# Moving the run-time branch of a fused attention and mixture-of-experts kernel ahead of the weight folds

## The reference

```
k_ids = jnp.arange(lk)[None, None, :]
qs = seg_id[:, :, None]
good = (k_ids <= qs) & (k_ids >= qs - LOOKBACK)
scores = jnp.where(good[:, None, :, :], scores, NEG)
attn = jax.nn.softmax(scores, axis=-1)
```

## Time and profile before

| | us |
|---|---|
| three runs, in order | 519.15, 522.25, 518.19 |
| median of the runs | 519.15 |
| the profiled execution | 518.47 |
| span of its profile, first to last instruction | 516.7 |
| TensorE busy | 499.3 |
| VectorE busy | 249.6 |
| ScalarE busy | 185.2 |
| GpSimd busy | 60.3 |

### The profile page before, as it was taken

One profiled execution on the slowest core, in us unless ns is written; L12 is line 12 of the kernel. 1 busy time (PEld: TensorE's weight loads), 2 busy tenths in 40 slices (PEclk: granted clock), 3 DMA queues, 4 the chain that ended last, 5 costly groups with the idle time before them and its releaser, 6 DMA issues.

```text
span 516.7 us, 10575 instructions
## 1 busy us (share of the span) xinstructions
PE 499.3 (97%) x3878; PEld 363.5 (70%) x3878; DVE 249.6 (48%) x549; ACT 185.2 (36%) x534; POOL 60.3 (12%) x71
## 2 busy tenths in 40 slices
PE   8699999999999999997999998999999999999997
PEld 7476777777877788885798885555555555556886
DVE  2565876876766668987553221222222222222334
ACT  2157567566566444444411111112112112121110
POOL 2000000000000122132006500000000000000650
PEclk9799999999999999999999999999999999999999
DMA  9800000000991009400523162777877877852241
GB/s 289 321 22 1 20 22 1 19 20 15 362 410 48 2 17 408 189 0 1 209 98 126 70 220 90 269 264 279 306 270 283 310 261 291 301 210 82 80 125 41
DMA packets 24455, 82.05 MB, mean 159 GB/s; under 512 B 2880, under 2 KB 16512, under 8 KB 20320
## 3 DMA queue, kind: packets, MB, share of 16 engines
q1 hardware_dynamic: 21536, 75.93, 40.3%
q0 software_dynamic: 1536, 4.20, 2.6%
q10 hardware_dynamic: 1344, 1.38, 0.8%
HBM read 73.10 MB, written 8.39 MB: 158 GB/s over the span
## 4 chain that ended last, share of the span: by engine, by line
PE 88%; DVE 6%; issue 3%; ACT 2%; POOL 0%; DVEq 0%; ACTq 0%; POOLq 0%
PE ps L1808 17%; PE ps L1721 12%; PE ps L1317 12%; PE ps L1832 9%; PE ps L1733 6%; PE ps L1396 5%; PE ps L1346 5%; PE ps L1365 5%; PE ps L1488 3%; PE ps L1384 3%; ACT w_routed L1096 1%; PE ps L1322 1%; PE ps L1498 1%; PE ps L1677 1%; PE ps L1338 1%
## 5 line engine op out<-in xcount | busy, mean ns | idle before, releaser
L1808 PE MATMUL ps<-w_routed,xnT 128*64 x320 | 93.8, 436 | 1.6 <-DVE x_sb L967 1.6
L1721 PE MATMUL ps<-xT_all,w_shared 128*128 128x256 f32 x320 | 75.7, 380 | 0.0
L1808 PEld LDWEIGHTS ps<-w_routed,xnT 128*64 128x64 f32 x320 | 42.0, 137 | 38.4 <-issue 27.2
L1721 PEld LDWEIGHTS ps<-xT_all,w_shared 128*128 128x128 f32 x320 | 60.3, 190 | 8.4 <-issue 0.4
L1096 ACT ACTIVATE w_routed<-ps,neg_top 128x128 f32<-128x128 f32 x128 | 45.1, 379 | 15.8 <-DVE neg_top L637 15.8
L1317 PEld LDWEIGHTS ps<-consts_a,w_routed 128*128 128x128 f32 x336 | 38.8, 145 | 15.2 <-issue 12.1
L1317 PE MATMUL ps<-consts_a,w_routed 128*128 128x128 f32 x336 | 46.2, 283 | 2.4 <-DVE x_sb L565 1.4
L1832 PE MATMUL ps<-w_routed,hidT 128*64 x200 | 47.4, 384 | 0.0
L1808 PE MATMUL ps<-w_shared,xnT 128*64 128x384 f32 (+1 forms) x160 | 46.9, 436 | 0.0
L1808 PE MATMUL ps<-x_up,xnT 128*64 128x384 f32 (+1 forms) x160 | 46.9, 436 | 0.0
L1286 ACT COPY hidT<-ps 128x384 f32<-128x384 f32 x20 | 9.6, 479 | 100.7 <-PE ps L1317 100.7
(11 more groups left out here) (181 smaller groups left out, 870.6 us busy)
## 6 DMA issues: line engine op xcount, KB each, us to landing
w_routed<-in_w_routed SPq DMA_DIRECT2D x8, 1920.0 KB, 14.4
x_up<-in_w_routed SPq DMA_DIRECT2D x10, 1280.0 KB, 5.9
w_shared<-in_w_routed SPq DMA_DIRECT2D x10, 1280.0 KB, 6.1
b_down<-in_w_routed SPq DMA_DIRECT2D x10, 640.0 KB, 5.7
w_shared<-in_w_routed SPq DMA_DIRECT2D x10, 640.0 KB, 5.4
w_shared<-in_w_shared SPq DMA_DIRECT2D x1, 3840.0 KB, 11.7
w_shared<-in_w_uvo SPq DMA_DIRECT2D x1, 2560.0 KB, 15.4
x_slots<-sil SPq DMA_DIRECT2D x16, 160.0 KB, 2.1
```

The lines of the kernel that those rows point to most:

```text
L1721: last = pe.matmul(ps[:, UP_BANK[m], half_ * D:(half_ + 1) * D].rearrange("p (n t) -> p n t", n=2), w_shared[:, j, at:at + P], xT_all[:, i ...
L1808: last = pe.matmul(ps[rows, b, 0:hi - lo], xnT[:, k, rows], w, start=k == 0, stop=k == KT - 1)
```

## The change

Four things are done, on all five engines together:

- The branch (`general`) moves ahead of everything that waits for a weight. TensorE: two warming products, before them the flag product, then the branch, then `WARM_UP - 4` (five) further warming products, the folds and the front of tile 0. VectorE: comparison of the segment numbers, the flag, the branch, and only then statistics, normalising, the mask and the rotations. ScalarE: the branch, then the evictions. GpSimd: the branch, then `rstd` of tiles 0 and 1.
- The segment numbers become ACT's first transfer instead of its third.
- The general path can no longer count on folds done before it. It makes its own, so its code grows by 16 and two products and two evictions; with the inputs used none of this is executed. `general` waits for other semaphores inside the `If`, which are not reached either.
- Warming products fall from nine to seven.

```diff
         def _(act):
             x_tiles = dram["x"].rearrange("(n p) d -> p n d", p=P)
+            act.dma_start(seg_i[:], dram["seg"]).then_inc(seg_in, 16)
             act.dma_start(x_sb[:, 0:2, :], x_tiles[:, 0:2, :]).then_inc(x0_in, 16)
             act.dma_start(consts_a[:], dram["consts_a"]).then_inc(const_in, 16)
-            act.dma_start(seg_i[:], dram["seg"]).then_inc(seg_in, 16)
             act.dma_start(x_sb[:, 2:, :], x_tiles[:, 2:, :]).then_inc(x_in, 16)
```

```diff
             pe.wait_ge(zero_set, 1)
-            keep_warm(WARM_UP)
-            pe.wait_ge(wu_in, 16)
-            for h in range(H):
-                last = pe.matmul(ps[0:QC, 2 + h // 8, ...], w_uq[:, h, :], w_uk[:, h, :],
-                                 start=True, stop=True)
-            last.then_inc(absorb_q_ps, 1)
-            pe.wait_ge(wk_in, 16 * 2)
-            ...
-            last.then_inc(absorb_k_ps, 1)
-            pe.wait_ge(const_in, 16)
-            xT(0)
-            qc(0)
             pe.wait_ge(flag_set, 1)
             pe.matmul(ps[0:1, 5, 0:1], half[:, 0:1], far_n[:], start=True, stop=True).then_inc(flag_ps, 1)
-            pe.wait_ge(absorb_k, 1)
-            pe.wait_ge(absorb_q, 1)
-            kv(0)
-            y_lat(0)
-            pe.wait_ge(wr_q_in, 16)
-            y_rope(0)
+            keep_warm(2)
...
             general(pe, g_tile, g_first)
+            keep_warm(WARM_UP - 4)
+            pe.wait_ge(wu_in, 16)
+            fold_q_work().then_inc(absorb_q_ps, 1)
+            pe.wait_ge(wk_in, 16 * 2)
+            fold_k_work().then_inc(absorb_k_ps, 1)
+            pe.wait_ge(const_in, 16)
+            xT(0)
+            qc(0)
+            pe.wait_ge(absorb_k, 1)
+            pe.wait_ge(absorb_q, 1)
+            kv(0)
+            y_lat(0)
+            pe.wait_ge(wr_q_in, 16)
+            y_rope(0)
+
             k_T(0)
```

```diff
-            dve.wait_ge(x0_in, 16)
-            dve.wait_ge(ones_set, 7)
-            for i in range(2):
-                stats(i).then_inc(mv_ready, 1)
...
-            normed(0, 1, xn, xT_ps, xn_ready, 0)
-
-            dve.wait_ge(const_in, 16)
+            dve.wait_ge(ones_set, 7)
             dve.wait_ge(seg_in, 16)
             link(dve.tensor_copy(seg[:], seg_i[:]))
             ...
             dve.tensor_reduce(far_n[:], far[:], AX.X, ALU.max).then_inc(flag_set, 1)
             link(dve.tensor_scalar(seg[:], seg[:], -LOOKBACK / 2, None, ALU.add))
-            ... (dist and win)
             dve.wait_ge(flag_ps, 1)
             dve.tensor_scalar(far_i[:], ps[0:1, 5, 0:1], -2.0, 1.0, ALU.mult, ALU.min).then_inc(far_ready, 1)
-            front_k(0, link)
-            front_rotate(0)
-            front_rotated(0)
...
             general(dve, g_tile, None, g_clear)
+            dve.wait_ge(x0_in, 16)
+            for i in range(2):
+                stats(i).then_inc(mv_ready, 1)
+            normed(0, 1, xn, xT_ps, xn_ready, 0)
+
+            dve.wait_ge(const_in, 16)
+            ...
+            front_k(0, link)
+            front_rotate(0)
+            front_rotated(0)
+
             front_qt(0)
```

More of the change, by code:

```diff
@@ L73 @@
 TAIL = {"divide": 2, "uT": 1, "uT_out": 1, "project": 1, "join": 4, "power2": 1, "keep": 1}
-FIRST = {"fold": 1, "fold_out": 1}
+FIRST = {"fold_q": 1, "fold_q_out": 1, "fold_k": 1, "fold_k_out": 1, "fold": 1, "fold_out": 1}
 CLEAR = {"clear": 1}
@@ L337, in general @@
                 eng.wait_ge(x_in, 16)
+                eng.wait_ge(wu_in, 16)
+                eng.wait_ge(wk_in, 16 * 2)
+                eng.wait_ge(wr_q_in, 16)
                 eng.wait_ge(wv_in, 16)
[L339 to L343, removed]
+                eng.wait_ge(const_in, 16)
+                eng.wait_ge(ctx_in, 16 * TB)
+                eng.wait_ge(ones_set, 7)
                 if first is not None:
@@ L504, in _ @@
             general(pool, g_tile)
+            for i in range(2):
+                rstd_of(i, i + 1)
             rstd_of(2, 3)
@@ L793, in _ @@
             general(dve, g_tile, None, g_clear)
+            dve.wait_ge(x0_in, 16)
+            for i in range(2):
+                stats(i).then_inc(mv_ready, 1)
+            normed(0, 1, xn, xT_ps, xn_ready, 0)
+            dve.wait_ge(const_in, 16)
+            link(dve.tensor_tensor(dist, keypos[:].unsqueeze(1).to_broadcast([P, NT, P]),
+                                   seg[:].unsqueeze(2).to_broadcast([P, NT, P]), ALU.subtract))
+            link(dve.tensor_tensor(dist, dist, dist, ALU.mult))
+            dve.tensor_scalar(win[:], dist, (LOOKBACK / 2) ** 2, -NEG, ALU.is_gt, ALU.mult).then_inc(win_ready, 1)
+            front_k(0, link)
+            front_rotate(0)
+            front_rotated(0)
             front_qt(0)
@@ L1204, in g_tile, with fold_q_out, fold_k_out @@
                 stage.end(last)
+            def fold_q_out():
+                return act.copy(w_q[:, 0].rearrange("p h c -> p (h c)"), ps[0:QC, 2:4, :].rearrange("p b n -> p (b n)"))
+            def fold_k_out():
+                return act.copy(w_k[:, :, KVC:], ps[:, 6, 0:KT * R].rearrange("p (k r) -> p k r", r=R))
             def g_first():
+                for name, work in (("fold_q_out", fold_q_out), ("fold_k_out", fold_k_out)):
+                    stage = Stage(act, "FIRST", name, 0)
+                    stage.end(work())
                 stage = Stage(act, "FIRST", "fold_out", 0)
@@ L1210, in _ @@
             general(act, g_tile, g_first)
+            act.wait_ge(absorb_q_ps, 1)
+            fold_q_out().then_inc(absorb_q, 1)
+            act.wait_ge(absorb_k_ps, 1)
+            fold_k_out().then_inc(absorb_k, 1)
+            xT_out(0)
+            qc_out(0)
+            kv_raw_out(0)
+            lat_out(0)
             k_out(0)
@@ L1638, in g_tile, with fold_q_work, fold_k_work @@
                 stage.end(project_work())
+            def fold_q_work():
+                for h in range(H):
+                    last = pe.matmul(ps[0:QC, 2 + h // 8, (h % 8) * KVC:(h % 8 + 1) * KVC], w_uq[:, h, :], w_uk[:, h, :],
+                                     start=True, stop=True)
+                return last
+            def fold_k_work():
+                for k in range(KT):
+                    last = pe.matmul(ps[:, 6, k * R:(k + 1) * R], w_kvcT[:, k * P:(k + 1) * P], w_kr[:], start=True, stop=True)
+                return last
             def g_first():
+                for name, work in (("fold_q", fold_q_work), ("fold_k", fold_k_work)):
+                    stage = Stage(pe, "FIRST", name, 0)
+                    stage.end(work())
                 stage = Stage(pe, "FIRST", "fold", 0)
```

16 lines of the change are left out of this document (removed).

## The result

The kernel after the change takes 529.13 us (median of 6 runs, 528.33 to 529.51), beside 519.39 us for the kernel before (6 runs, 518.19 to 522.25): 1.0186 times as long, interval 1.0167 to 1.0205, so 1.9% slower. The profiled execution took 529.44 us with a span of 527.6, against 516.7: +10.9 us. The forecast was 527.0 (521.5 to 530.0), slower.

A forecast was written before the change was run, and what follows sets the result against it. TensorE, busy 97% of the span, was taken to bound the kernel. The query transposes of tile 0 start 9.3 us later, minus 1.4 if the clock stays up: 519.15 + 7.9 = 527.0 us, range 521.5 to 530.0.

The forecast's parts named there:

- segment numbers arrive, cast: ACT's first transfer lands at 6.9 us and VectorE's cast runs then; bounds 2.9 and 7.9.
- far_ready: The flag is ready at 8.0 us, after 0.7 of VectorE operations and 0.4 for TensorE's product and hand-overs.
- length of the branch: TensorE's COMPARE_BRANCH at 8.9 us fetches its target's code by DMA and takes 5.0 us.
- folds to the end of the rotation: Front of tile 0: 13.43 us as in the kernel before, plus 0.4 for folds at half clock.
- q_T(0): Query transposes of tile 0 on TensorE start at 32.0 us instead of 22.73, +9.3.
- given back by the clock up to the first maximum: Query transposes, xn transposes and part of the scores run at full clock if it stays up: 1.4 us less.
- likeliest case: Total time 524.5 to 528.5 us, with a branch stall of 3 to 6.3 us and the clock up or down.
- the longer rival: TensorE's branch takes the full 6.3 us (+1.3) and the clock falls before the query transposes (+1.4): 529.7 us, chance 0.12.
- Less a shorter wait for a turn: TensorE's branch: the earlier 6.3 us lowered to 5.0 for a shorter wait of its instruction packet in the DMA queues.
- The +0.4 for folds at half clock: About one microsecond of the folds on TensorE runs before the clock rises, costing 0.4 us.
- The free branch: TensorE's branch target is at hand, stall 0.05 us, folds at 13.3: 522.1 us, chance 0.11.
- the early segment numbers: ACT's segment numbers land at 2.9 us, all else as forecast: 523.0 us, chance 0.12.

The follow-up runs named there:

- combined: Kernel before with flag decided earlier, w_uvo, consts_b and a_w held back, five warming products before k_T(0), ACT's transfer order as before: 517.98 us against 519.02.
- after_late_loads: Kernel after with SyncE issuing w_uvo, consts_b and a_w only once the first fold is done: 529.45 us, ratio 1.0191.
- after_no_warm: Kernel after without the five warming products behind the branch: 530.28 us, ratio 1.0215.
- after_short_aligned: Kernel after with the code TensorE's branch skips shortened by exactly 512 instructions, per-tile work of the general path replaced by filler: 522.15 us, ratio 1.0051.
- after_quiet_start: Kernel after with w_uvo, consts_b, a_w and the x of tiles 2 to 7 held back behind the folds: 531.39 us, ratio 1.0214.

## Why the prediction was right, and where its sizes were off

**Direction and mechanism held, but for the clock.** The stall moved with the branch and lost its cover; the segment numbers did not come early; the warming products cost their 4.4 us; the shift went to the end one to one. By its own steps, forecast against the trace of after:

| step | forecast | trace |
|---|---|---|
| segment numbers arrive, cast | 6.9 | 6.82 |
| `far_ready` | 8.0 | 8.1 |
| TensorE's branch | 8.9 | 9.0 |
| length of the branch | 5.0 | 7.74 |
| TensorE goes on | 13.9 | 16.75 |
| folds | 18.2 | 21.13 |
| folds to the end of the rotation | 13.83 | 13.12 |
| `q_T(0)` | 32.0 | 34.39 |
| given back by the clock up to the first maximum | 1.4 | 0.74 |

The last entry is (28.55 - 22.73) - (39.47 - 34.39) = 0.74. The forecast of the shift was 9.3 - 1.4 = 7.9; the trace has 11.66 - 0.74 = 10.92. That the time came as near as 529.13 against 527.0 is in part luck: the median rose by 9.7, the profiled execution by 11.0. And 529.13 lies outside the 524.5 to 528.5 that the prediction gave its likeliest case; it is the longer rival that carries the range so far.

**The term that was mis-sized is the branch**, 5.0 forecast and 7.74 measured. "Less a shorter wait for a turn" was the failing step: I lowered the 6.3 of the earlier trace rows by 1.3 with no row that showed a shorter queue. Stretches of the kernel before, which I could have read for it, have the DMA engines as busy at 9 us as at 16 or busier (the share is the last number but one):

```profile
16.00:19.00 3.00, 1.73 (x5) 0.42 (x3) 1.23 (x2) 1.01 (x1) 0.00 (x0) 1.00 0.93 383
...
9.00:12.00 3.00, 2.83 (x29) 2.45 (x27) 1.69 (x10) 1.09 (x3) 1.08 (x2) 1.00 1.06 284
```

In the kernel after the share is 1.15 in 9 to 13 us, and the two queues moved 606 packets each. The wait for the packet was 4.8 us instead of 3.6, longer and not shorter. So 6.3 was no bound from above either, being the price of one stretch; it runs from 3.5 to 7.7 over these kernels.

**The step that failed is the clock.** I wrote that `k_T(0)` now runs inside the wait for the rotation and leaves only 3.3 us of idleness. It waits for VectorE's last reading of `y_rope`, L597, as the row at 33.13 says, so it runs 2.6 us after `y_rope` and 0.85 before the transposes. That is 3.45 us of idleness, about as forecast, and the clock fell all the same, just behind it: the sixteen transposes took 3.33 us. TensorE worked at 0.50 for about 3.4 us (34.7 to 38.1) instead of 5.0 (22.5 to 27.5), so half of the 1.4 came back. What kept it up was filler, in `combined` (1.94).

**Two smaller ones.** The +0.4 for folds at half clock did not appear: the ten records of the five warming products were enough to bring the clock up by 21.13 (in `after_late_loads` not quite, 3.48 us of folds), and `after_no_warm` shows the price without them. The other engines' branches could have stalled up to 6 us by my text; they took 45 to 67 ns, and VectorE's next wait was for `x_sb`, which came 1.7 us later than before and not 0.5. Neither reached the end, as TensorE's stall covered both.

**Among the rivals**, "longer" (529.7, with 0.12) came nearest: both its parts occurred, the stall beyond its 6.3 and the clock in half. The free branch and the early segment numbers are excluded, by the 7.74 us and by the cast at 6.82. The Trainium skill's figure of about 2 us for a small transfer, which the prediction set beside the early numbers, stands in a section headed for transfers of GpSimd; ACT's 4 KB took 6.0 us here beside `w_uqk`. The 522.15 of `after_short_aligned` is what the free branch gives, and the forecast for it was 522.1; that it is so close is partly luck, as `q_T(0)` came 0.5 us earlier than that rival said and the clock gave back some 0.6 instead of 1.4.

**What stays open.** The fetch takes 7.2 to 7.7 us in the kernel after and 6.2 to 6.3 in the old place. By the table above nearly all of that lies ahead of the packet, 4.3 to 4.8 us against 3.6, in queues that are full both times, and I cannot say why it has to wait longer in the one. Two packets of q14 come with TensorE's in the kernel after, where before it was the only one in 19 to 21 us; but they come with it in `after_quiet_start` too, where it waited 1.8 us only. That later code suffers by its place in the blocks rests on two kernels, one shifted by 638 instructions and one by 512. And no run tried the change with its warming products ahead of the flag.

## What to carry to other kernels

On TensorE a branch over 500 instructions or more was a DMA here, not an instruction: look for COMPARE_BRANCH by engine, and price it by whether its target is near and by what is queued on the DMA engines at that moment. Put it where the engine would wait anyway; in front of the first useful work it is paid in full. Before taking idle or filler work in front of a chain for a loss or a gain, ask what clock the work behind will see, and change the length of code only with an eye on what it shifts.

## What the runs showed of the hardware that I had not expected

- TensorE's branch took 0.23 to 0.38 us with its target within some 270 instructions, and 3.5 to 7.7 us where it jumped over 500 or more; 523 and 783 cost the same. The Trainium skill, Runtime: NRT & Kernel Launch, "Instruction fetch mechanics", gives TensorE room for 2048 instructions and most engines two blocks; here a target 523 instructions ahead was not at hand. How much room TensorE has is not shown by that: no q8 packet had moved from the start of the span to 13.8 us, so no fetch further ahead shows before the branch either.
- The fetch waits while data are queued: 7.7 us in full queues, 4.9 as they emptied, 3.5 and 3.7 where SyncE's transfers were held back. From the packet to the end of the branch it was 2.6 to 3.1 us in all of them, full queues or empty, and from the branch to the packet 0.8 to 4.8.
- Straight-line code can starve as well: behind 127 records of products of 8 columns in 1.24 us TensorE stood idle for 2.23 us, with an instruction packet in that time, when the code in front of them was 638 instructions shorter, and not when it was 512 shorter.
- 4 KB in 128 rows took 6.0 us as the first transfer of its queue, and delayed the 256 KB behind it by 2.0 us in the kernel before.
- With five warming products in front TensorE worked at the lower level for 4.4 us; in `after_no_warm`, with the folds in their place, for some 11.
- Ten filler records, 2.3 to 2.4 us of TensorE, kept the clock at 1.00 across a wait where without them it fell, and 16 transposes took 1.94 us instead of 3.16.
